# Paced row scatters, paired gathers and column-tiled expert matmuls in an attention and mixture-of-experts kernel

## The chip, the core and the metric

The kernel runs on one core of one Trainium2 chip. The metric is the device time of one execution in microseconds (us); before the change the median of three runs is 681.27 us (680.93 to 682.08).

## What is computed

One transformer layer on x of 1 x 2048 x 128, all in float32. x is normalised, and two branches are added to it.

```
xn = layernorm(x)
attention: 16 heads of width 8; q, k, v = xn W * mod
  w = softmax(q k^T / sqrt(8) * cos(2 pi (i - j) / 2048)) over j
  w = (w + roll(w, 1)) / sqrt(2);  out = (w v) Wo
experts:   logits over 8 experts per token; the best 2 are taken, softmax over the 2
  for each taken pair (token, expert e):
    a, g = split(xn w1[e]^T)       # 352 + 352 columns
    y = (silu(a) * g) w2[e]^T      # 128 columns, times the pair's score
out = x + attention + sum of the token's two y
```

## The kernel before, in words

**Attention** sets the order of the work. 16 heads are taken one after the other. A head has 64 score tiles of 128 keys by 512 queries; a score tile is one f16 matmul of 49 rows (line 1253) into a PSUM bank. Five banks form a ring, filled in groups of 3 and 2 tiles. ACT takes each group with one exponential (line 652) into `probs`. Four finished tiles make a set (a "quad" in the code, w = 0 to 255, 16 to a head), and `weighted_values` (line 1270) multiplies a set with the head's values: four matmuls, each on a column tile of 32 columns of the array, each with a moving operand of 512 columns. A float32 matmul stands in the trace as two, and a float32 transpose as one. Each set raises `pv_done`.

**Rounds** carry everything else. A round is 5 score tiles, so 1.25 sets, and there are 205. In a round PE issues the two score groups, then at most one or two maximum jobs (`max_job`, for the two heads with an exact shift), then one expert step, then the sets that have become ready. `scores(g)` waits until ACT has finished group g - 2.

**Experts.** The 4096 token and expert pairs are sorted by expert into 39 tiles of 128 slots. Slots and owners come from `assign_slots` in round 8. POOL then scatters the normalised rows into slot order in DRAM (`slots_x`, line 550): 32 indirect DMAs of 128 rows. Before the change they come in two runs of 16 with nothing between the DMAs of a run; between the runs POOL waits for `pv_done` of 16 and copies head 2's values into `vh` (line 532). After the last it clears `qe`, which shares memory with the rows (line 557).

Expert tile m takes three steps in three rounds, and two tiles take 7 rounds, from round `EXPERTS_AT` on (`expert_step`): step 0 is `result(m - 1)` (line 1198, 3 matmuls) and `turn_rows(m)` (line 1179, one transpose), steps 1 and 2 are `widen` (line 1189, 3 matmuls each). All of them use the full 128 by 128 array with 128 moving columns. ACT adds one tanh to step 1 (line 644), DVE copies between steps (lines 901 to 923).

**SP** loads each head's operands (`load_head`, 10 DMAs, lines 352 to 401), asks for the first expert rows and weights in its program order at round `EXPERTS_AT` - 2 (lines 410, 429, 430), and for the exact heads' operands at `EXPERTS_AT`.

**Gathers.** The 39 results go to DRAM (`slots_y`). From set `GATHER_AT` on POOL brings them back in token order with 32 indirect DMAs (line 536), one per set, each after `pv_done` of w. DVE adds them in head 15 from its set 4 on, w = 244, and needs all 32.

**Maximum jobs.** 64 of them, `JOBS_A_HEAD` to a head from head `FIRST_JOB_HEAD` on; heads 14 and 15 need the result.

Of the kernel before, what the change touches and what calls it, by code (L numbers as in the profile page):

```python
# [37 lines left out]
P = 128  # L38
S = 2048
DM = 128  # L40
H = 16
D = 8
E = 8
F = 352
NT = S // P
# [23 lines left out]
EXACT = 2  # L69
PLAIN = H - EXACT  # L70
JOBS = EXACT * NT * 2
FIRST_JOB_HEAD = 3
JOBS_A_HEAD = 7
JOB_QUAD = 4
PAIR_EXP_AT = 3
TOP_EXP_AT = 12
RANK_AT = 8
SECOND_AT = 9
EXPERTS_AT = 26
ROUNDS_A_PAIR = 7  # L80
SQUARES_AT = (4, 5)
HALF_HEADS = H // 2
EARLY = HALF_HEADS - EXACT
GATHER_AT = 206
ISQ8 = float(1.0 / np.sqrt(D))
TWO_PI = 2.0 * np.pi
PI_A = 6.28125
# [19 lines left out]
def build(nc, x, Wq, Wk, Wv, Wo, phase, amp, wqkv, w1, w2, ident_in, desc_in, cs_in, sel_in, tri_in, below_in, count_in, heads_in, earlier_in, out):  # L107
# [11 lines left out]
    with ExitStack() as ctx:  # L119
# [393 lines left out]
        def _(pool):  # L513
# [31 lines left out]

            pool.wait_ge(xn_ready, NT)
            pool.wait_ge(slot_ready, 1)
            for r in range(2):
                for t in range(NT):
                    nc.gpsimd.indirect_dma_start(slots_x, bass.IndirectOffsetOnAxis(ap=slot[:, r, t:t + 1], axis=0),  # L550
                                                 xn[:, t, :], None).then_inc(scattered, 16)
                if r == 0:
                    pool.wait_ge(pv_done, QUADS)
                    head_values(2)

            pool.wait_ge(scattered, 2 * NT * 16)
            nc.gpsimd.memset(qe[:], 0.0).then_inc(rows_ready, 1)

            for w in range(2 * QUADS, H * QUADS):
                if w % QUADS == 0 and w // QUADS + 1 < H:  # L560
                    pool.wait_ge(pv_done, w)
                    head_values(w // QUADS + 1)
                j = w - GATHER_AT
                if j == 0:
                    for half in range(2):
                        pool.wait_ge(y_wr[half], ROW_PAIRS // 2 * 16)
                    pool.wait_ge(scratch_wr, 16 * 16)
                    pool.wait_ge(norm_parts, 4)
                if 0 <= j < 2 * NT:
                    pool.wait_ge(pv_done, w)  # L570
                    gather_result(j)

        @block.scalar
        def _(act):
# [490 lines left out]
        def _(pe):  # L1065
# [105 lines left out]
            def turn_rows(m):  # L1171

                pe.wait_ge(xg_ld[m // 2 % 2], m // 4 * 16 + 16)
                after(pe, xgT_ready, m)
                if m == 0:
                    pe.wait_ge(order_ready, 2)
                    pe.wait_ge(slot_ready, 1)
                after(pe, hidT_ready, m)
                nc.tensor.transpose(ps[:, SIDE_BANK, 0:P], xg[:, m % 4, :], ident[:]).then_inc(xgT_ps, 1)  # L1179

            def widen(m, b, ready):

                pe.wait_ge(staged_ld[m % STAGES], (m // STAGES + 1) * 32)
                pe.wait_ge(xgT_ready, m + 1)
                after(pe, y_copied, m)
                if b == 1:
                    pe.wait_ge(a_taken, m + 1)
                for f, (f0, n) in enumerate(FCH):
                    ins = nc.tensor.matmul(ps[0:n, SIDE_BANK, P * f:P * f + P],  # L1189
                                           w1_of[m % STAGES][:, F * b + f0:F * b + f0 + n],  # L1190
                                           xgT[:, m % 2, :], start=True, stop=True)
                ins.then_inc(ready, 1)

            def result(m):
                pe.wait_ge(hidT_ready, m + 1)
                after(pe, y_copied, m)
                for f, (f0, n) in enumerate(FCH):
                    ins = nc.tensor.matmul(ps[:, SIDE_BANK, FP:FP + DM], hidT[0:n, m % 2, f, :],  # L1198
                                           w2_of[m % STAGES][0:n, f, :], start=f == 0, stop=f == NF - 1)
                ins.then_inc(y_ready, 1)  # L1200

            def expert_work(r):
# [210 lines left out]
```

## Time and profile before

| | |
|---|---|
| median of 3 runs | 681.27 us |
| the profiled execution, its own time | 681.02 us |
| its span in the profile | 679.1 us |
| mean granted TensorE clock | 0.961 of full |
| PE busy | 595.2 us, 88% |
| ACT busy | 524.2 us, 77% |
| POOL busy | 81.7 us, 12% |

Times in the trace are microseconds from the start of the span. A row of a timeline is a stretch of instructions of one line: start, length, engine, line, operation, operands, count, and in brackets how long the engine had been idle and what ended that. "remote" or "another core or an unknown queue" means that the event that released the engine could not be matched to an instruction that had just finished. PEld is the loading of weights into the array, which overlaps PE.

### The profile page before, as it was taken

Reading aid. Unit: us, or ns where it says so; the run is one execution under the profiler, and the core shown is the slowest. Engines: PE = TensorE matmul, PEld = TensorE weight load, DVE = VectorE, ACT = ScalarE, POOL = GpSimd, SP = SyncE. Lnnn points to the kernel's source line nnn. Section 1 sums busy time; section 2 is a strip of 40 time slices with the busy share of each in tenths; the row PEclk is TensorE's granted clock in tenths of the full one; section 3 lists DMA queues with packets and bytes.
Section 4 is the critical chain, followed back from the end, with each engine's and each line's share of the span. In section 5 each row is a group of like instructions: output and inputs, shape, how many; then the busy total and the mean of one; then the engine's idle time right before and its main releaser. Section 6 shows DMA issues by size and latency. Waiting matters only on the chain.

```text
span 679.1 us, 11462 instructions
## 1 busy us (share of the span) xinstructions
PE 595.2 (88%) x4181; PEld 209.4 (31%) x4181; DVE 199.2 (29%) x491; ACT 524.2 (77%) x489; POOL 81.7 (12%) x94
## 2 busy tenths in 40 slices
PE   2887766389999999999999999999999998888985
PEld 1341111013333334333333333333333331211213
DVE  6675511002123232323333232332323220000233
ACT  2649945398888788887887888888878889999992
POOL 4100176500000000000000000000000003455000
PEclk9997787599999999999999999999999999999999
DMA  8345122404322224132131322223222100111002
GB/s 236 117 131 171 42 65 67 134 22 130 115 77 82 84 76 117 52 106 68 58 117 60 100 75 84 82 60 99 83 77 82 44 9 21 36 33 34 9 1 65
DMA packets 42813, 52.99 MB, mean 78 GB/s; under 512 B 7245, under 2 KB 32359, under 8 KB 42499
## 3 DMA queue, kind: packets, MB, share of 16 engines
q1 hardware_dynamic: 39616, 47.71, 23.4%
q0 software_dynamic: 2048, 4.20, 2.1%
q8 instruction: 36, 0.59, 0.3%
q10 hardware_dynamic: 1090, 0.30, 0.3%
q14 instruction: 23, 0.18, 0.1%
HBM read 38.54 MB, written 13.63 MB: 77 GB/s over the span
## 4 chain that ended last, share of the span: by engine, by line
PE 58%; ACT 18%; issue 15%; another core or an unknown queue 3%; DVE 2%; DMA 1%; ACTq 1%; SPq 0%; DVEq 0%
PE ps L1270 25%; PE ps L1253 16%; ACT big L652 15%; PE ps L1189 7%; PE ps L1198 5%; ACT cs L644 2%; PE ps L1087 2%; PE ps L1277 1%; PE ps L1287 1%; ACTq L578 1%; PE ps L1179 1%; PE ps L1228 1%; DMA ang<-L_attn_quantum_amplitude 1%; PE ps L1075 1%
## 5 line engine op out<-in xcount | busy, mean ns | idle before, releaser
L652 ACT ACTIVATE big<-ps 128x1536 f32<-128x1536 f32 (+1 forms) x410 | 482.0, 1245 | 114.3 <-PE ps L1253 89.8
L1270 PE MATMUL ps<-big,vh 128*32 128x512 f32 x2048 | 269.5, 616 | 0.0
L1253 PE MATMUL ps<-qa,ka 49*128 49x512 f16 x896 | 164.9, 395 | 52.0 <-ACT big L652 42.0
L1253 PEld LDWEIGHTS ps<-qa,ka 49*128 49x128 f16 x896 | 39.3, 94 | 256.2 <-ACT big L652 221.2
L1189 PE MATMUL ps<-xgT,store 128*128 128x128 f32 (+1 forms) x468 | 72.5, 291 | 0.0
L961 DVE TENSOR_REDUCE m<-ps 128x1 f32<-128x512 f32 x64 | 44.3, 692 | 94.0 <-PE ps L1287 94.0
L1270 PEld LDWEIGHTS ps<-big,vh 128*32 128x32 f32 x2048 | 45.6, 109 | 75.3 <-issue 60.5
L1189 PEld LDWEIGHTS ps<-xgT,store 128*128 128x128 f32 (+1 forms) x468 | 55.7, 181 | 28.2 <-issue 28.2
L532 POOL COPY vh<-vaug 128x144 f32 x16 | 5.1, 319 | 433.8 <-PE ps L1270 407.6
L908 DVE SCALAR_TENSOR_TENSOR cs<-cs,ps 128x384 f32<-128x384 f32 x39 | 21.6, 554 | 75.0 <-ACT cs L644 75.0
L901 DVE COPY xgT<-ps 128x128 f32<-128x128 f32 x39 | 11.4, 292 | 92.0 <-PE ps L1179 92.0
L536 POOL DMA_INDIRECT store<-slots_y,slot x32 | 30.5, 954 | 57.7 <-PE ps L1270 54.5
L550 POOL DMA_INDIRECT slots_x<-attnT,slot x32 | 31.3, 980 | 44.6 <-DVE slot L888 35.1
L1198 PE MATMUL ps<-store,cs 128*128 128x128 f32 (+1 forms) x234 | 36.4, 292 | 0.0
L1198 PEld LDWEIGHTS ps<-store,cs 128*128 128x128 f32 (+1 forms) x234 | 29.0, 190 | 13.3 <-issue 13.3
L917 DVE SCALAR_TENSOR_TENSOR cs<-cs,ps 128x384 f32<-128x384 f32 x39 | 21.6, 554 | 35.5 <-PE ps L1189 35.0
L1253 PE MATMUL ps<-attnT,ka 49*128 49x512 f16 x128 | 24.4, 384 | 7.9 <-ACT big L652 7.0
L944 DVE COPY osb<-ps 128x512 f32<-128x512 f32 x16 | 11.0, 687 | 68.2 <-PE ps L1270 67.5
L1287 PE MATMUL ps<-ka,attnT 49*128 49x512 f16 x64 | 24.1, 376 | 0.0
L644 ACT ACTIVATE cs<-ps 128x384 f32<-128x384 f32 x39 | 18.9, 485 | 0.0
L1087 PE MATMUL ps<-xnT,wmat 128*64 128x512 f32 x64 | 18.6, 677 | 0.0
L1253 PEld LDWEIGHTS ps<-attnT,ka 49*128 49x128 f16 x128 | 5.7, 93 | 38.3 <-ACT big L652 34.4
(164 smaller groups left out, 231.8 us busy)
## 6 DMA issues: line engine op xcount, KB each, us to landing
store<-in_L_ffn_w SPq DMA_DIRECT2D x39, 352.0 KB, 3.0
store<-in_L_ffn_w SPq DMA_DIRECT2D x39, 192.0 KB, 3.1
qk_parts<-store SPq DMA_DIRECT2D x16, 256.0 KB
qa<-qk_parts SPq DMA_DIRECT2D x27, 128.0 KB
slots_x<-vh SPq DMA_DIRECT2D x5, 512.0 KB, 6.2
cs<-slots_x SPq DMA_DIRECT2D x20, 128.0 KB, 3.1
slots_y<-y SPq DMA_DIRECT2D x19, 128.0 KB, 3.1
ka<-qk_parts SPq DMA_DIRECT2D x31, 64.0 KB, 2.2
```

The costliest lines, as they stand in the source:

```text
L536: nc.gpsimd.indirect_dma_start(gathered[:, r, t, :], None, slots_y, bass.IndirectOffsetOnAxis(ap=slot[:, r, t:t + 1], axis=0)).then_inc(ga ...
L550: nc.gpsimd.indirect_dma_start(slots_x, bass.IndirectOffsetOnAxis(ap=slot[:, r, t:t + 1], axis=0), xn[:, t, :], None).then_inc(scattered, 16)
L644: nc.scalar.activation(turned_gate[:, m % 2, :], ps[:, SIDE_BANK, 0:FP], ACT.Tanh, scale=0.5).then_inc(gate_ready, 1)
L652: nc.scalar.activation(probs[:, prob_of(tiles[0]):prob_of(tiles[-1]) + 1, :], ps[:, bank_of(tiles[0]):bank_of(tiles[-1]) + 1, :], ACT.Exp, ...
L908: nc.vector.scalar_tensor_tensor(turned_gate[:, k, :], turned_gate[:, k, :], 1.0, ps[:, SIDE_BANK, 0:FP], ALU.add, ALU.mult).then_inc(a_ta ...
L961: nc.vector.tensor_reduce(m4[:, NT * r + i, c:c + 1], ps[:, O_BANKS[(p - 1) % 2], :], AX, ALU.max).then_inc(m_reduced, 1)
L1087: ins = nc.tensor.matmul(ps[64 * half:64 * half + 64, PROJ_BANKS[n % 4], :], wmat[:, which, 64 * g:64 * g + 64], xnT[:, CW * c:CW * c + CW ...
L1189: ins = nc.tensor.matmul(ps[0:n, SIDE_BANK, P * f:P * f + P], w1_of[m % STAGES][:, F * b + f0:F * b + f0 + n], xgT[:, m % 2, :], start=Tru ...
L1198: ins = nc.tensor.matmul(ps[:, SIDE_BANK, FP:FP + DM], hidT[0:n, m % 2, f, :], w2_of[m % STAGES][0:n, f, :], start=f == 0, stop=f == NF - 1)
L1253: ins = nc.tensor.matmul(ps[:, bank_of(n), :], k[at:at + KQ, P * o:P * o + P], q[at:at + KQ, CW * c:CW * c + CW], start=True, stop=True, t ...
L1270: ins = nc.tensor.matmul(ps[32 * c:32 * c + 32, O_BANKS[p % 2], :], vh[:, p % 2, o + 8 * b, :], probs[:, prob_of(n), :], start=k == 0, sto ...
L1287: nc.tensor.matmul(ps[:, O_BANKS[(p - 1) % 2], :], qe[at:at + KQ, r, P * i:P * i + P], near_keys(ka[at:at + KQ, 2 + r, :], i), start=True, ...
```

## The change

1. The 32 row scatters are issued one by one, each after a further set of value matmuls (w = 16 to 47); the clearing of `qe` follows at w = 48, ahead of head 4's values.
2. Expert steps start in round 41 instead of 26, so that they end in round 177 instead of 162. The maximum jobs go 8 to a head over heads 4 to 11 instead of 7 to a head over heads 3 to 12.
3. Gathers start at set 224 instead of 206, two to a set.
4. Each expert matmul, and the transpose of the rows, becomes several matmuls of 32 columns on the array's four column tiles: a widening step has 4 + 4 + 3 instead of 3, a result 12 instead of 3, the transpose becomes 4 ordinary matmuls with the identity. Per expert tile 38 matmuls stand in place of 10.

```diff
--- before.py
+++ after.py
@@ -69,19 +69,21 @@
 EXACT = 2
 PLAIN = H - EXACT
 JOBS = EXACT * NT * 2
-FIRST_JOB_HEAD = 3
-JOBS_A_HEAD = 7
+FIRST_JOB_HEAD = 4
+JOBS_A_HEAD = 8
 JOB_QUAD = 4
 PAIR_EXP_AT = 3
 TOP_EXP_AT = 12
 RANK_AT = 8
 SECOND_AT = 9
-EXPERTS_AT = 26
+EXPERTS_AT = 41
+SCATTER_AT = 16
 ROUNDS_A_PAIR = 7
 SQUARES_AT = (4, 5)
 HALF_HEADS = H // 2
 EARLY = HALF_HEADS - EXACT
-GATHER_AT = 206
+GATHER_AT = 224
+GATHERS_A_QUAD = 2
 ISQ8 = float(1.0 / np.sqrt(D))
 TWO_PI = 2.0 * np.pi
 PI_A = 6.28125
@@ -545,22 +547,23 @@
 
             pool.wait_ge(xn_ready, NT)
             pool.wait_ge(slot_ready, 1)
-            for r in range(2):
-                for t in range(NT):
-                    nc.gpsimd.indirect_dma_start(slots_x, bass.IndirectOffsetOnAxis(ap=slot[:, r, t:t + 1], axis=0),
-                                                 xn[:, t, :], None).then_inc(scattered, 16)
-                if r == 0:
-                    pool.wait_ge(pv_done, QUADS)
-                    head_values(2)
-
-            pool.wait_ge(scattered, 2 * NT * 16)
-            nc.gpsimd.memset(qe[:], 0.0).then_inc(rows_ready, 1)
-
-            for w in range(2 * QUADS, H * QUADS):
+            def scatter_rows(j):
+                r, t = j // NT, j % NT
+                nc.gpsimd.indirect_dma_start(slots_x, bass.IndirectOffsetOnAxis(ap=slot[:, r, t:t + 1], axis=0),
+                                             xn[:, t, :], None).then_inc(scattered, 16)
+
+            for w in range(SCATTER_AT, H * QUADS):
+                i = w - SCATTER_AT
+                if i < 2 * NT:
+                    pool.wait_ge(pv_done, w)
+                    scatter_rows(i)
+                if i == 2 * NT:
+                    pool.wait_ge(scattered, 2 * NT * 16)
+                    nc.gpsimd.memset(qe[:], 0.0).then_inc(rows_ready, 1)
                 if w % QUADS == 0 and w // QUADS + 1 < H:
                     pool.wait_ge(pv_done, w)
                     head_values(w // QUADS + 1)
-                j = w - GATHER_AT
+                j = GATHERS_A_QUAD * (w - GATHER_AT)
                 if j == 0:
                     for half in range(2):
                         pool.wait_ge(y_wr[half], ROW_PAIRS // 2 * 16)
@@ -568,7 +571,8 @@
                     pool.wait_ge(norm_parts, 4)
                 if 0 <= j < 2 * NT:
                     pool.wait_ge(pv_done, w)
-                    gather_result(j)
+                    for k in range(GATHERS_A_QUAD):
+                        gather_result(j + k)
 
         @block.scalar
         def _(act):
@@ -1176,7 +1180,10 @@
                     pe.wait_ge(order_ready, 2)
                     pe.wait_ge(slot_ready, 1)
                 after(pe, hidT_ready, m)
-                nc.tensor.transpose(ps[:, SIDE_BANK, 0:P], xg[:, m % 4, :], ident[:]).then_inc(xgT_ps, 1)
+                for c in range(0, DM, 32):
+                    ins = nc.tensor.matmul(ps[c:c + 32, SIDE_BANK, 0:P], xg[:, m % 4, c:c + 32], ident[:], start=True, stop=True,
+                                           tile_position=(0, c))
+                ins.then_inc(xgT_ps, 1)
 
             def widen(m, b, ready):
 
@@ -1186,17 +1193,19 @@
                 if b == 1:
                     pe.wait_ge(a_taken, m + 1)
                 for f, (f0, n) in enumerate(FCH):
-                    ins = nc.tensor.matmul(ps[0:n, SIDE_BANK, P * f:P * f + P],
-                                           w1_of[m % STAGES][:, F * b + f0:F * b + f0 + n],
-                                           xgT[:, m % 2, :], start=True, stop=True)
+                    for c in range(0, n, 32):
+                        ins = nc.tensor.matmul(ps[c:c + 32, SIDE_BANK, P * f:P * f + P],
+                                               w1_of[m % STAGES][:, F * b + f0 + c:F * b + f0 + c + 32],
+                                               xgT[:, m % 2, :], start=True, stop=True, tile_position=(0, c))
                 ins.then_inc(ready, 1)
 
             def result(m):
                 pe.wait_ge(hidT_ready, m + 1)
                 after(pe, y_copied, m)
                 for f, (f0, n) in enumerate(FCH):
-                    ins = nc.tensor.matmul(ps[:, SIDE_BANK, FP:FP + DM], hidT[0:n, m % 2, f, :],
-                                           w2_of[m % STAGES][0:n, f, :], start=f == 0, stop=f == NF - 1)
+                    for c in range(0, P, 32):
+                        ins = nc.tensor.matmul(ps[c:c + 32, SIDE_BANK, FP:FP + DM], hidT[0:n, m % 2, f, c:c + 32],
+                                               w2_of[m % STAGES][0:n, f, :], start=f == 0, stop=f == NF - 1, tile_position=(0, c))
                 ins.then_inc(y_ready, 1)
 
             def expert_work(r):
```

## Rows read from the trace of the kernel before

**Rows 1.** the page: engines' busy time, granted clock in 40 slices, chain that ended last.
```profile
...
PE 595.2 (88%) x4181; PEld 209.4 (31%) x4181; DVE 199.2 (29%) x491; ACT 524.2 (77%) x489; POOL 81.7 (12%) x94
...
PEclk9997787599999999999999999999999999999999
...
PE 58%; ACT 18%; issue 15%; another core or an unknown queue 3%; DVE 2%; DMA 1%; ACTq 1%; SPq 0%; DVEq 0%
```

**Rows 2.** waits between 60 and 140 us: total us, times, longest.
```profile
...
ACT big L652 <- remote: 24.2, 4, 13.2
...
DVE weight_sums L952 <- remote: 15.0, 1, 15.0
DVE rank L775 <- remote: 9.7, 1, 9.7
```

**Rows 3.** timeline 72 to 136 us (start, length, engine, line), and one window's sums.
```profile
...
80.91 1.16 POOL L550 DMA_INDIRECT slots_x<-attnT,slot  x1 [35.15 <-DVE slot L888]
...
90.56 0.39 PE L1253 MATMUL ps<-qa,ka 49*128 49x512 f16 x2 [0.31 <-issue]
...
94.60 1.45 ACT L652 ACTIVATE big<-ps 128x1536 f32<-128x1536 f32 x1 [4.10 <-remote]
...
100.18 1.18 POOL L550 DMA_INDIRECT slots_x<-attnT,slot  x1 [0.30 <-issue]
...
105.53 0.98 POOL L550 DMA_INDIRECT slots_x<-attnT,slot  x1 [0.34 <-issue]
...
115.26 0.82 PE L1253 MATMUL ps<-qa,ka 49*128 49x512 f16 x5
...
124.61 0.96 POOL L550 DMA_INDIRECT slots_x<-attnT,slot  x1 [0.30 <-issue]
...
128.38 2.37 ACT L652 ACTIVATE big<-ps 128x1536 f32<-128x1536 f32 x2 [13.21 <-remote]
...
106.00:130.00 24.00, 10.70 (x66) 2.26 (x64) 1.14 (x6) 9.21 (x9) 18.11 (x17) 0.71 0.21 66
```

**Rows 4.** windows, ACT's line 652 alone: one stretch with, one without expert steps.
```profile
...
163.00:557.00 394.00, 312.04 (x264) 1.00 0.27 81
563.00:655.00 92.00, 85.59 (x76) 1.00 0.09 24
```

**Rows 5.** timeline 300 to 322 us, PE: value, widening and result matmuls.
```profile
...
300.45 1.92 PE L1270 MATMUL ps<-big,vh 128*32 128x512 f32 x16
...
303.05 0.93 PE L1189 MATMUL ps<-xgT,store 128*128 128x128 f32 x6
...
303.91 1.06 PE L1270 MATMUL ps<-big,vh 128*32 128x512 f32 x8
...
305.68 0.94 PE L1198 MATMUL ps<-store,cs 128*128 128x128 f32 x6
...
306.66 1.07 PE L1270 MATMUL ps<-big,vh 128*32 128x512 f32 x8
```

**Rows 6.** the same timeline at 81.8 us: the densest matmuls of the trace.
```profile
...
81.82 0.54 PE L1108 MATMUL ps<-sel,second 128*128 128x8 bf16 x16 [2.00 <-DVE sel L749]
```

**Rows 7.** SP's issues of one head's load (timeline), and median landing times (page).
```profile
...
301.06 0.33 SPq L352 DMA_DIRECT2D qa<-qk_parts  x1
...
305.21 0.24 SPq L401 DMA_DIRECT2D qa<-shift_rows  x1
...
store<-in_L_ffn_w SPq DMA_DIRECT2D x39, 352.0 KB, 3.0
...
cs<-slots_x SPq DMA_DIRECT2D x20, 128.0 KB, 3.1
```

**Rows 8.** timeline, POOL: gathers at one to a set of value matmuls.
```profile
...
594.51 0.95 POOL L536 DMA_INDIRECT store<-slots_y,slot  x1 [1.31 <-PE ps L1270]
595.76 0.95 POOL L536 DMA_INDIRECT store<-slots_y,slot  x1 [0.30 <-issue]
597.11 0.95 POOL L536 DMA_INDIRECT store<-slots_y,slot  x1 [0.40 <-PE ps L1270]
```

## The prediction

> **What bounds the kernel now.** I read the page first. PE is busy 88% of the span, ACT 77%, and the chain that ended last is 58% PE and 18% ACT [rows 1]. So matmuls set the time, but not everywhere, and 3% of the chain belongs to nobody: "another core or an unknown queue". The granted clock is at 9 tenths or more in 35 of 40 slices and lower in slices 4 to 8, about 51 to 136 us [rows 1]. Two questions follow: what happens there, and what sets the pace of a round elsewhere.
>
> The waits of 60 to 140 us answer the first. ACT stands still 24.2 us in 4 waits whose releaser is unknown, and DVE 15.0 and 9.7 us in one wait each [rows 2]. The timeline tells who is late. The scores of 90.56 us are done in 0.39 us, yet ACT takes them at 94.60; the scores of 115.26 us are taken at 128.38, 13.21 us of idle ACT [rows 3]. DVE's two waits are for PE as well. So a signal that PE sends arrives microseconds late. What runs beside it is POOL's scatters: 16 in a row from 80.91 to about 101.4, and 16 from 105.53 to 125.6, at a pitch of 1.27 us ((100.18 - 80.91) / 15 is 1.28) [rows 3]. The first stall begins some 10 us after its run of scatters began, the second likewise, and the last one ends 2.8 us after the last scatter. My reading: scatters that follow each other without a pause hold up PE's signals after about eight of them. Around the stalls PE also runs at a reduced clock, 0.71 on average from 106 to 130 us [rows 3], though slice 4 shows that the clock was low before the first scatter.
>
> For the second question I count ACT's exponentials, two to a round. With expert steps 132 rounds take 394 us, 2.98 us each; without, 38 rounds take 92 us, 2.42 each, and there ACT's line 652 alone is busy 85.6 of 92 [rows 4]. So rounds without expert work are ACT's, those with it are PE's, and an expert step costs time because it stands in PE's order between scores and value matmuls.
>
> **The scatters.** Spaced, they need a pitch of one set. A round is 1.25 sets, so a set is 2.42 / 1.25 = 1.94 us; POOL's 1.27 us fits. The gathers of the kernel before have just that spacing, with at most three in a row (594.51, 595.76, 597.11) [rows 8], and no unknown wait stands beside them. So the stalls should go: ACT's 24.2 less some 0.7 that it would have idled anyway, **-23.5 us**. Bounds: 0 if spacing does not help, -24.2. With no stall the clock should recover sooner: PE was busy 10.7 us at 0.71 in one window [rows 3], of which full clock saves at most 3.1, and the first stall is like it; between 0 and 6 I take **-2**, as half of the slow matmuls stood beside ACT's work and the clock was low before. What waits instead: `vh` of heads 2 and 3 is copied after one scatter of 1 us, and is needed 16 sets (31 us) later; the clearing of `qe` at w = 48 and head 4's copy behind it have the same 31 us, and the exact heads' operands are wanted only in round 55. All cost nothing while rounds take 2.4 us.
>
> **The later start of the experts.** The same 137 rounds carry them. The maximum jobs lie in 8 heads instead of 10; each needs PE's place in a round and its count stays 64. Between 0 and 2 us I take **+1**. New is that the first rows are wanted soon after the last scatter. Count from the start T of round 38. SP first waits for its first score group (0.6), reads a register (about 1), and issues head 4's ten DMAs, which take 4.4 us [rows 7]. The last scatter starts when set 46 is done, T + 2, and has landed by T + 4.4, so SP, not POOL, is late. The rows are asked for at T + 6 and land 3.1 us later [rows 7], at T + 9; PE wants them in round 41 after its scores, 3 x 2.42 + 0.8 = T + 8.1. The first weights (3.0 us to land [rows 7]) come behind them, at T + 11, wanted at T + 10.5. PE waits once for about 1 us, between 0 and 3: **+1**. Its sets and ACT queue behind that wait.
>
> **The gathers.** They must be in by w = 244 and start at w = 224. Two of them are 2.5 us (0.95 + 0.30 each [rows 8]) against 1.94 us of a set, so POOL falls behind and works 40 us without a pause; 20 sets are 39 us. They land 3 us after DVE could begin adding. 32 additions of 0.3 us, about 10, then still end before head 15 does at w = 256, 23 us after w = 244. By itself that costs 0. What a pauseless run may do is a rival below.
>
> **The column tiles.** Now 6 full-array matmuls of a widening step start at 303.05 and the next value matmuls at 303.91: 0.86 us. A result with the transpose of the next rows takes 305.68 to 306.66: 0.98 [rows 5]. The value matmuls show what column tiles do. One set is eight matmuls of 512 columns in 1.06 us, two sets 1.92, so four matmuls on four column tiles advance together at 0.86 / 2 = 0.43 us [rows 5]. With 128 columns, four should take a quarter, 0.107; I take 0.109. The widening step becomes 3 chunks x 2 passes = 6 such groups: 0.65, and 0.02 for the first load, 0.68. That is no faster as arithmetic: the full array paces at the same rate. What goes is the switch: in a step's last 0.2 us the array drains before the value matmuls can load; in the same tiling they follow at once, and their own first load (0.02) hides too. Saved per widening step 0.86 - 0.68 + 0.02 = 0.20. The result has 6 groups too, but the transpose grows from one pass to two: 0.68 + 0.22 = 0.90, saved 0.98 - 0.90 + 0.02 = 0.10. PE saves 78 x 0.20 + 39 x 0.10 = 19.5 us.
>
> Not all of it shows. Per two tiles (7 rounds) expert steps take PE 4 x 0.86 + 2 x 0.98 = 5.4 us, but the rounds are longer by only 7 x 0.56 = 3.9, or 72% of it: ACT's pace hides the rest. I take 70%, **-14 us**; all of it would be -19.5, none 0.
>
> **Sum.** The profiled execution took 681.0 us (span 679.1 and 1.9 around it), within 0.3 of the median of 681.3. 681.0 - 23.5 - 2 + 1 + 1 - 14 = 643.5, and against the median 644.
>
> **Rivals.**
> (a) *The paired gathers bring the stall back.* POOL then issues 32 without a pause, as in the scatters' runs. For: same kind of instruction, same pitch of 1.25 to 1.27 us [rows 3, 8]. Against: they write to the core, not to DRAM, and POOL waits for PE before each pair, so a stall throttles its own cause. Worked out: PE goes on for 9 us (4.6 sets), POOL needs 11.5 for their pairs, and signals recover some 2 us after it stops. About 4.6 us are lost for 4.6 sets, three times in 16 sets: 14 us, **658**.
> (b) *Spaced scatters stall PE too*, as the cause is the scatters' number and not their pitch. Half of the stalls left: **656**; all: 669.
> (c) *The column tiles save nothing.* The densest matmuls here are 16 in 0.54 us, 0.034 each with its load [rows 6]. If that is the floor, a widening step's 22 take 0.75 (saved 0.1) and result and turn, 32, take 1.09 (lost 0.1): PE saves 4 us, 3 show, **655**.
> (d) *PE's issue becomes the bound: slower.* The 0.034 was seen over 16 pairs only, which may have been queued while PE stood still; over a longer stretch the trace shows no more than 8 pairs in 0.86 us, 0.107 each [rows 5]. 39 tiles issue 39 x (2 x 22 + 32) = 2964 pairs where 105 us were spent. At x us a pair the steps cost 2964 x - 105; at 0.044 this eats the scatters' 25.5, beyond it the kernel is slower. Taken at 0.05: 681 - 25.5 + 43 + 2 = **701**. Against: rows 5's second set follows at the array's pace, and rows 6.
>
> The Trainium skill, "TensorE: Matmul & The Clock Gate", section "Wait — 56ns, not 53.3ns?", says that with hardware decoding off the sequencer spends about 62 ns on each matmul, which binds once the array's work per matmul is shorter. By that page 2964 pairs would be 184 us, an estimate, and the kernel would take about 736 us; the 0.034 of rows 6 speaks against it.
> (e) *The change does not do what it says*, say the sets no longer line up with the expert steps or a load comes much later than I count: 5 us or more on top.
>
> **How the numbers follow.** Forecast (643.5 to 644, own range 637 to 650) 0.48; (a) 0.24; (b) 0.10; (c) 0.09; (d) 0.05; (e) 0.04. The low end takes the whole 19.5 us of PE and a bit more clock: 637, with 1 to spare 636. The high end must hold (a), (b) at half and (c), with their spread: 664. Outside are (d), the full (b) and part of (e). About 0.2% (1.4 us) is what can be told from no change. All cases but (d) are faster by far: faster 0.94, same 0.01, slower 0.05. The predicted time is the likeliest case's, 644.
>
> **What the changed profile would show.** Scatters right: one per 1.9 us, no unknown wait of ACT, and a clock above 0.83 from 100 us on. Widening right: 22 matmul records (44 a tile), six groups at 0.11 us, and value matmuls 0.68 us after the step's start; at 1 us or more (d) is true, at 0.75 (c). Rounds with expert steps should take 2.88 us, those without 2.42. A wait of PE for rows or weights of about 1 us stands at round 41. In the gathers' stretch the round tells (a): 2.42, or over 2.9 with unknown waits. The prediction is wrong if the sets do not follow an expert step at once, if scatters at a pitch of 1.9 us still delay PE's signals, or if the saved PE time turns into waits for ACT.

## The result, and the profile after

| | before | after |
|---|---|---|
| median | 681.56 us of 4 runs (680.93 to 682.08) | 658.24 us of 4 runs (657.71 to 662.35) |
| ratio | | 0.967, 95% interval 0.963 to 0.971 |
| the profiled execution | 681.02 us | 657.95 us |
| its span | 679.1 us | 656.0 us |

The kernel is 23.3 us faster. That lies inside the predicted range (636 to 664), but not at the likeliest case, 644: it is the number of rival (a), 658.

The page of the kernel after: busy times, clock in 40 slices of 16.4 us, POOL's slices, the chain that ended last.

```profile
PE 576.5 (88%) x6404; PEld 211.0 (32%) x6404; DVE 202.2 (31%) x491; ACT 523.8 (80%) x489; POOL 81.6 (12%) x94
...
POOL 4200014445000000000000000000000000266200
PEclk9987789999999999999999999999999999977999
...
PE 56%; ACT 19%; issue 17%; DMA 2%; SPq 2%; DVE 2%; ACTq 1%; another core or an unknown queue 1%; DVEq 0%
```

Against [rows 1]: PE has 2223 more matmuls and is busy 18.7 us less. The 3% of the chain that belonged to nobody are now 1%. The clock's dip ahead of 98 us (slices 3 to 6) is still there; a second one has appeared in slices 36 and 37 (574 to 607 us), under POOL's second busy stretch. That is where to look.

First the two stretches that the change was meant for. Waits of 60 to 140 us: the largest of POOL and DVE, and ACT's only line (total us, times, longest):

```profile
POOL slots_x L552 <- PE ps L1279: 69.8, 18, 49.0
...
DVE osb L948 <- PE ps L1279: 24.1, 1, 24.1
...
ACT big L656 <- PE ps L1262: 6.5, 8, 1.3
```

No wait there has an unknown releaser any more; [rows 2] had 24.2 us of them on ACT alone. The sums of 98 to 140 us, of before and of after, show the same (each fence: busy us and count of each engine, then granted clock, DMA share, GB/s):

```profile
98.00:140.00 42.00, 22.77 (x130) 4.49 (x132) 5.45 (x19) 19.45 (x17) 22.05 (x21) 0.69 0.29 91
```

```profile
98.00:140.00 42.00, 36.91 (x261) 7.99 (x259) 1.96 (x7) 38.25 (x34) 20.13 (x23) 1.00 0.16 48
```

34 exponentials in place of 17. The granted clock is 1.00 (2.4 GHz) in place of 0.69; in the trace before it stood at 0.50 (1.2 GHz) from 97 to 110 us, after ACT's first wait, and again from 121 to 134, in the longest wait and behind it.

The column tiles, in PE's timeline of a widening step and of a result with its transpose:

```profile
298.99 0.75 PE L1197 MATMUL ps<-xgT,store 128*32 128x128 f32 x19
299.47 0.62 PE L1279 MATMUL ps<-big,vh 128*32 128x512 f32 x1
299.56 0.28 PE L1197 MATMUL ps<-xgT,store 128*32 128x128 f32 x3
299.67 1.89 PE L1279 MATMUL ps<-big,vh 128*32 128x512 f32 x15
...
304.87 0.86 PE L1207 MATMUL ps<-store,cs 128*32 128x128 f32 x24
305.55 0.40 PE L1184 MATMUL ps<-ident,cs 128*32 128x128 f32 x8
305.77 1.04 PE L1279 MATMUL ps<-big,vh 128*32 128x512 f32 x8
```

The widening step has 22 records and gives way to the value matmuls after 299.67 - 298.99 = 0.68 us, where it took 0.86 [rows 5]; result and transpose take 305.77 - 304.87 = 0.90, where they took 0.98. Both are the numbers of the prediction. One value matmul even starts at 299.47, inside the step: the last chunk of 96 columns uses three column tiles, which leaves the fourth to it (that it is the fourth is inferred; the rows do not name the tile).

Then the exponentials of ACT's line 656 in three windows (two to a round): with expert steps, beside the gathers, and behind them.

```profile
170.00:555.00 385.00, 314.48 (x267) 1.00 0.28 83
564.00:612.00 48.00, 32.13 (x28) 0.86 0.16 42
614.00:638.00 24.00, 22.82 (x21) 1.00 0.02 4
```

385 / 133.5 is 2.88 us a round, as forecast. Behind the gathers it is 24 / 10.5 = 2.3 (2.42 was forecast; the window's edges cut rounds, and 12 whole rounds, 192 to 204, take 2.44 each). Between them stands what the forecast's likeliest case did not have: 48 us for 14 rounds, 3.4 us each. Fourteen rounds should take 34. The waits of 560 to 656 us name it:

```profile
ACT big L656 <- remote: 9.5, 4, 3.3
...
POOL store L538 <- remote: 6.7, 3, 2.4
```

And the timeline of the first of these waits, all engines, with some rows left out:

```profile
573.21 2.37 ACT L656 ACTIVATE big<-ps 128x1536 f32<-128x1536 f32 x2 [0.34 <-PE ps L1262]
...
574.72 0.60 PE L1262 MATMUL ps<-attnT,ka 49*128 49x512 f16 x3 [0.33 <-issue]
...
575.63 0.39 PE L1262 MATMUL ps<-attnT,ka 49*128 49x512 f16 x2 [0.31 <-ACT big L656]
576.05 0.95 POOL L538 DMA_INDIRECT store<-slots_y,slot  x1 [0.30 <-issue]
577.31 0.95 POOL L538 DMA_INDIRECT store<-slots_y,slot  x1 [0.30 <-issue]
578.48 1.45 ACT L656 ACTIVATE big<-ps 128x1536 f32<-128x1536 f32 x1 [2.90 <-remote]
578.57 0.95 POOL L538 DMA_INDIRECT store<-slots_y,slot  x1 [0.30 <-issue]
579.83 0.95 POOL L538 DMA_INDIRECT store<-slots_y,slot  x1 [0.30 <-issue]
...
582.99 0.95 POOL L538 DMA_INDIRECT store<-slots_y,slot  x1 [2.21 <-remote]
```

The group of three score tiles begun at 574.72 (128x1536 for ACT) is done by about 575.3. ACT, idle from 575.58, takes it at 578.48. The group of two begun at 575.63 is done by about 576.0, and ACT takes it at 580.58, 4.6 us later. The gathers began at 568.44 and follow each other every 1.26 us; the tenth starts at 579.83, and then POOL itself waits for PE's late signal. ACT and POOL are released together, at 582.90 and 582.99, some 2 us after the tenth gather ended. The trace also keeps the semaphores' updates: four of PE's, for work that had ended up to several us earlier, come within 0.2 us there (582.73 to 582.92). So the signals look queued: they come late and one by one while the gathers run, and in a burst once POOL pauses. The trace has four such runs (10, 10, 10 and 2 gathers) and three stalls, beginning six or seven gathers into a run: the picture of [rows 3], cut into pieces.

The stall has a second price. Behind the first two of the three, PE runs at half clock (0.50, which is 1.2 GHz) for a while; it had been busy for 3.5 of the 7 us from 575 to 582, ahead of the first such stretch. A part of that stretch, with all engines (the other is 596 to 602.5 us):

```profile
583.00:588.00 5.00, 4.45 (x20) 0.66 (x17) 0.00 (x0) 4.62 (x4) 3.80 (x4) 0.50 0.14 39
```

To see where all of the 23 us went I counted rounds by the starts of ACT's exponentials in four traces: before and after; the kernel after on another chip (e16, below); and before with the column tiles alone (e2, below). Microseconds of each stretch (rounded, so sums can be 0.1 off):

| rounds | before | after | e2, tiles alone | e16, after on another chip |
|---|---|---|---|---|
| 0 to 8 | 25.8 | 25.2 | 25.7 | 25.7 |
| 8 to 20, the scatters | 60.0 | 33.7 | 33.5 | 38.2 |
| 20 to 178, all expert steps | 461.4 | 449.3 | 449.0 | 449.3 |
| 178 to 182 | 9.8 | 10.9 | 9.8 | 11.0 |
| 182 to 192, gathers paired | 24.4 | 38.5 | 24.4 | 24.4 |
| 192 to 204 | 29.3 | 29.3 | 29.3 | 29.3 |

Before to after: -0.6 - 26.3 - 12.1 + 1.1 + 14.1 = -23.8; the first exponential came 0.7 us later, so -23.1, which is the difference of the spans. The change won 38.4 us in two places and gave 14.1 back in ten rounds. ACT's unknown waits are 9.5 of the 14.1; most of the rest is ACT waiting for PE with a known releaser, where PE runs at half clock and catches up (ACT is idle 14.7 us in these ten rounds, and 1.6 before).

### The profile page after: what moved, and what is told of

Its sections match the earlier page's. It is cut to its first block, busy times and chain, and to the rows that moved or that the text cites. A ratio compares the mean times of both kernels' runs of the same rounds, so it can differ in the third digit from the quotient of the medians.

```text
span 656.0 us, 15907 instructions
## 1 busy us (share of the span) xinstructions
PE 576.5 (88%) x6404; PEld 211.0 (32%) x6404; DVE 202.2 (31%) x491; ACT 523.8 (80%) x489; POOL 81.6 (12%) x94
## 3 DMA queue, kind: packets, MB, share of 16 engines
q1 hardware_dynamic: 39616, 47.71, 24.4%
## 4 chain that ended last, share of the span: by engine, by line
PE 56%; ACT 19%; issue 17%; DMA 2%; SPq 2%; DVE 2%; ACTq 1%; another core or an unknown queue 1%; DVEq 0%
PE ps L1279 23%; PE ps L1262 16%; ACT big L656 16%; PE ps L1197 5%; PE ps L1207 5%; ACT cs L648 2%; PE ps L1091 2%; PE ps L1184 1%; PE ps L1286 1%; PE ps L1296 1%; ACTq L582 1%; PE ps L1237 1%; PE ps L1079 1%; PE ps L1101 1%
## 5 line engine op out<-in xcount | busy, mean ns | idle before, releaser
L1279 PE MATMUL ps<-big,vh 128*32 128x512 f32 x2048 | 280.8, 610 | 0.0
L1279 PEld LDWEIGHTS ps<-big,vh 128*32 128x32 f32 x2048 | 65.6, 109 | 52.2 <-issue 43.5
L1197 PE MATMUL ps<-xgT,store 128*32 128x128 f32 x1716 | 66.8, 277 | 0.4 <-DMA store<-in_L_ffn_w 0.4
L1197 PEld LDWEIGHTS ps<-xgT,store 128*32 128x32 f32 x1716 | 45.8, 109 | 27.9 <-issue 27.2
L1262 PE MATMUL ps<-attnT,ka 49*128 49x512 f16 x128 | 26.0, 414 | 17.6 <-ACT big L656 12.7
L1207 PE MATMUL ps<-store,cs 128*32 128x128 f32 (+1 forms) x936 | 33.7, 277 | 0.0
L921 DVE SCALAR_TENSOR_TENSOR cs<-cs,ps 128x384 f32<-128x384 f32 x39 | 21.6, 555 | 33.5 <-PE ps L1197 31.7
L1207 PEld LDWEIGHTS ps<-store,cs 128*32 128x32 f32 (+1 forms) x936 | 23.3, 110 | 13.2 <-issue 13.2
```

Source lines behind the costliest of these rows:

```text
L1197: ins = nc.tensor.matmul(ps[c:c + 32, SIDE_BANK, P * f:P * f + P], w1_of[m % STAGES][:, F * b + f0 + c:F * b + f0 + c + 32], xgT[:, m % 2, ...
L1207: ins = nc.tensor.matmul(ps[c:c + 32, SIDE_BANK, FP:FP + DM], hidT[0:n, m % 2, f, c:c + 32], w2_of[m % STAGES][0:n, f, :], start=f == 0, s ...
L1262: ins = nc.tensor.matmul(ps[:, bank_of(n), :], k[at:at + KQ, P * o:P * o + P], q[at:at + KQ, CW * c:CW * c + CW], start=True, stop=True, t ...
L1279: ins = nc.tensor.matmul(ps[32 * c:32 * c + 32, O_BANKS[p % 2], :], vh[:, p % 2, o + 8 * b, :], probs[:, prob_of(n), :], start=k == 0, sto ...
```

## The experiments

Twelve runs were made. They fell on several chips, and it turned out that the chip matters, so each time stands beside that of the kernel before on the same chip.

**1. The whole change without the column tiles.**

```diff
...
-                for c in range(0, DM, 32):
-                    ins = nc.tensor.matmul(ps[c:c + 32, SIDE_BANK, 0:P], xg[:, m % 4, c:c + 32], ident[:], start=True, stop=True,
-                                           tile_position=(0, c))
-                ins.then_inc(xgT_ps, 1)
+                nc.tensor.transpose(ps[:, SIDE_BANK, 0:P], xg[:, m % 4, :], ident[:]).then_inc(xgT_ps, 1)
...
```

(`widen` and `result` go back likewise.)

> The kernel after, with the transpose, the widening and the result matmuls of the experts back on the full array (10 matmuls a tile instead of 38). If column tiles save what the prediction says (0.20 us of PE per widening step, 0.10 per result, 70% of it shown), this takes 14 us more than the kernel after: about 672, and rounds with expert steps 2.98 instead of 2.90 us. If the column tiles save nothing (rival c) it takes 655 to 660, the same as the kernel after.

Measured: 656.88 us against 655.48 of before, ratio 1.003 (0.9995 to 1.006). The surprise is the second number: the kernel before, 681 us in the result, took 655 here. On this chip the stalls do not exist (the traces of 2 and 3 show it), and all of the change but the tiles is worth nothing. The forecast of 14 us between this kernel and the one after was borne out in part by experiment 3, on the same chip and with the same tiles and start of the experts as after: 645.21, 11.7 us less, and 13.4 us less in rounds 20 to 178 (449.3 against 462.7). With expert steps a round took 3.00 us:

```profile
170.00:555.00 385.00, 304.33 (x257) 1.00 0.29 85
```

**2. The column tiles alone**, put into the kernel before: the reverse of that edit.

> The kernel before with the column tiles alone. By the forecast 14 us less than before: about 667. If the gain depends on the other parts, or is nothing: 678 to 681. The stalls of 90 to 128 us stay as they were (ACT idle on unknown releasers about 24 us).

Measured on the same chip: 641.23 against 655.48, ratio 0.977 (0.974 to 0.980): -14.3 us. A round with expert steps, 330 / 114.5 = 2.88 us:

```profile
170.00:500.00 330.00, 269.05 (x229) 1.00 0.28 84
```

Its scatters still come in two runs of 16, at the pitch of [rows 3]. Here are their first ones, and the sums of the stretch that holds both runs:

```profile
82.68 0.98 POOL L550 DMA_INDIRECT slots_x<-attnT,slot  x1 [0.30 <-issue]
83.96 0.97 POOL L550 DMA_INDIRECT slots_x<-attnT,slot  x1 [0.30 <-issue]
```

```profile
80.00:126.00 46.00, 39.27 (x286) 8.77 (x289) 8.48 (x31) 42.76 (x39) 34.17 (x34) 0.96 0.21 66
```

ACT is busy 42.8 of 46 us, with no unknown wait. The same scatters, on another chip, cause no stall: a pauseless run of indirect DMAs does not suffice for it.

**3. The scatters back in two runs of 16, all else as after.**

```diff
-                if i < 2 * NT:
+                if i < 2 * NT and i % NT == 0:
                     pool.wait_ge(pv_done, w)
-                    scatter_rows(i)
+                    for k in range(NT):
+                        scatter_rows(i + k)
```

> The kernel after, with the 32 row scatters in two runs of 16 again (at sets 16 and 32). If it is the pauseless run that holds up PE's signals, two stalls come back beside them, 11 to 13 us each, and the time is 658 + 23 to 26 = 681 to 684. If it was the place in the kernel (the early rounds, their table loads and head order) that stalled and not the run, 658 to 661.

Measured: 645.21, ratio 0.985 (0.980 to 0.990), on the chip of the first two. No unknown wait in the scatters nor in the paired gathers, although all 32 gathers follow each other at 1.26 us here, in one row. A miss: it was written for a chip that stalls, and says nothing of the pitch. It took 4.0 us more than experiment 2, of which the later start explains 1.5 (below); its four times spread from 642.9 to 648.5, and the rest is not explained.

**4. One gather to a set.** So that they can start at set 204, the expert steps are packed into 6 rounds for two tiles in place of 7.

```diff
-ROUNDS_A_PAIR = 7
+ROUNDS_A_PAIR = 6
-GATHER_AT = 224
-GATHERS_A_QUAD = 2
+GATHER_AT = 204
+GATHERS_A_QUAD = 1
```

> The kernel after, with an expert step in every round (two tiles in 6 rounds instead of 7), so that the experts end 19 rounds earlier, and the gathers one to a set from set 204 on. If the paired gathers' pauseless run costs the 14 to 15 us of rival (a), this takes 642 to 644, with no unknown wait of ACT or POOL after 540 us. If the rounds of the last heads are slow for another reason (DVE's late additions, the exact heads), 655 to 658. If the denser expert steps cost more than the free rounds hid: 645 to 650.

Measured, still on that chip: 640.31, ratio 0.976 (0.972 to 0.979). Without stalls on the chip this does not tell the expectation's cases apart; it does show that the denser packing costs nothing (rounds 41 to 182 take 405.2 us, against 407.8 in experiment 3). The tiles alone (experiment 2) took 641.23 there, so on such a chip nearly all of the gain is theirs.

**5 and 6. After and before again, on another chip**, to find out whether the stalls are real and which chips have them.

> The kernel after, unchanged, since the kernel before took 655.5 us on the chip of the first four experiments and 681.6 on the chip of the result, and no unknown wait stood in their traces. If the stalls belong to some chips and not to others: on a chip where before takes 655, after takes 641 to 644, a ratio of 0.98, with no unknown waits beside its gathers; on a chip where before takes 681, after takes 658, ratio 0.967. If the gathers' stall is there on every chip: 655 to 658 even where before takes 655.

> The kernel before, unchanged, for its trace on this chip. If it takes 655: ACT has no wait on an unknown releaser between 80 and 130 us although the scatters stand in the same two runs of 16 at a pitch of 1.27 us, and rounds 8 to 20 take 33 to 34 us instead of 60. If it takes 681: the same stalls as in the first trace.

Measured: after 661.38, before 680.35, ratio 0.973 (0.969 to 0.978); before once more, 679.7. This chip stalls. Rounds 182 to 204 of the kernel after take 69.5 us in its trace, where a trace without stalls has 53.8: the gathers cost 15.7 us. Waits beside the gathers of the kernel after, then waits of 60 to 140 us of the kernel before:

```profile
ACT big L656 <- remote: 10.8, 3, 4.7
```

```profile
ACT big L652 <- remote: 24.8, 3, 13.2
DVE weight_sums L952 <- remote: 14.2, 1, 14.2
DVE rank L775 <- remote: 7.4, 1, 7.4
```

They are the sizes of the result's chip, so the stall is not chance. It goes with the chip: the experiments ran on five chips; three had the kernel before at 655 to 658 us, and no trace from them has such a wait; two had it at 680. (Whether the result's chip is one of these two is not known. Each chip was used in one session only, so the chip itself and its state in that session are not told apart.)

**7 and 8. One gather to a set, and gathers in two pauseless runs of 16**, both packed as in 4. The edit of 8, against 4:

```diff
...
-                if 0 <= j < 2 * NT:
+                if 0 <= j < 36 and j % 18 == 0:
                     pool.wait_ge(pv_done, w)
-                    for k in range(GATHERS_A_QUAD):
-                        gather_result(j + k)
+                    for k in range(16):
+                        gather_result(j // 18 * 16 + k)
```

> The same kernel as e4_single_gathers (an expert step in every round, gathers one to a set from set 204 on), since its first run fell on a chip without stalls. On a chip where before takes 680: if the paired gathers' pauseless run is the whole cause of the last stretch's loss, 641 to 644 and no unknown wait, a ratio of 0.943 to 0.947; if single gathers stall this chip too, 650 or more. On a chip where before takes 655: 640 again.

> The kernel of e4_single_gathers, but the gathers in two runs of 16 without a pause, at sets 204 and 222: as the scatters stood before, and at the same mean rate as single gathers. On a chip where before takes 680: if the length of a pauseless run is the cause, two stalls of ACT of about 11 us each, starting 6 to 10 us into each run, 662 to 668; if the mean rate is what counts, no stall, 641 to 644. On a chip where before takes 655: no stall, 640.

Measured: 642.25 against 658.18, ratio 0.977 (0.971 to 0.982), and 644.98 in a single run. The chip had no stalls, so 8 settles nothing.

**9. One gather to a set, a third time**, now on a chip that stalls (before 680.48).

> The same kernel as e4_single_gathers once more, as both runs of it fell on chips without stalls. Where before takes 680: 641 to 644 if every pauseless run is gone and single transfers don't stall (ratio 0.943 to 0.947), 650 or more if single ones do. Where before takes 655: 640 to 642.

Measured: 640.08, ratio 0.945 (0.938 to 0.952). No unknown wait in the whole trace. The stretch of the gathers:

```profile
530.00:610.00 80.00, 74.81 (x66) 1.00 0.10 25
```

80 / 33 = 2.42 us a round. On chips that stall, the kernel after lost 14 to 16 us in its gathers. POOL still issues up to four gathers in a row (behind the copy of `vh`), which is short enough:

```profile
532.53 0.97 POOL L538 DMA_INDIRECT store<-slots_y,slot  x1 [0.34 <-issue]
533.81 0.96 POOL L538 DMA_INDIRECT store<-slots_y,slot  x1 [0.30 <-issue]
535.07 0.95 POOL L538 DMA_INDIRECT store<-slots_y,slot  x1 [0.30 <-issue]
536.33 0.95 POOL L538 DMA_INDIRECT store<-slots_y,slot  x1 [0.30 <-PE ps L1279]
538.93 0.95 POOL L538 DMA_INDIRECT store<-slots_y,slot  x1 [1.65 <-PE ps L1279]
```

**10. Four patterns in one kernel**, on that chip: a pauseless run of 16 scatters, 16 scatters one to a set, 16 gathers with a small POOL operation (a memset of unused memory) behind each, and two pauseless runs of 8 gathers. Whichever stalls then stalls beside one that doesn't. The part of the edit on the gathers:

```diff
...
+                if j == 0:
+                    pool.wait_ge(pv_done, w)
+                    for k in range(NT):
+                        gather_result(k)
+                        nc.gpsimd.memset(pause[:, k, :], 0.0)
+                if j in (20, 30):
                     pool.wait_ge(pv_done, w)
-                    for k in range(GATHERS_A_QUAD):
-                        gather_result(j + k)
+                    for k in range(8):
+                        gather_result(NT + 8 * (j // 30) + k)
```

> The kernel of e4_single_gathers with four different spacings in one look. Scatters: 16 in a run at set 16, the other 16 one to a set from set 32. Gathers: 16 in a run at set 204, each followed by a POOL memset of some 0.4 us, so at a pitch of about 1.7 us; 8 in a run at set 224; 8 in a run at set 234. On a chip where before takes 680, if a pauseless run of more than about seven is the cause: unknown waits of ACT beside the scatters' run (about 11 us), none beside the scatters one to a set, none or up to 4 us beside each run of 8. If the pitch matters and not the number, none beside the paused gathers; if the number without a wait in between matters, about 11 us there too. On a chip where before takes 655: no unknown waits, 640 to 645.

Measured, a single run: 664.57 us. The pauseless scatters (97.96 to 118.2) hold ACT up twice. Timeline:

```profile
109.62 0.96 POOL L553 DMA_INDIRECT slots_x<-attnT,slot  x1 [0.30 <-issue]
110.77 2.36 ACT L666 ACTIVATE big<-ps 128x1536 f32<-128x1536 f32 x2 [5.76 <-remote]
110.89 0.96 POOL L553 DMA_INDIRECT slots_x<-attnT,slot  x1 [0.30 <-issue]
...
119.27 1.45 ACT L666 ACTIVATE big<-ps 128x1536 f32<-128x1536 f32 x1 [6.13 <-remote]
```

The windows of ACT's line 666 (busy, count, clock, DMA share, GB/s): pauseless scatters, scatters one to a set, paced gathers.

```profile
98.00:120.00 22.00, 10.10 (x10) 0.79 0.18 58
141.00:172.00 31.00, 28.58 (x26) 1.00 0.15 49
540.00:565.00 25.00, 23.27 (x21) 1.00 0.15 40
```

4.4 us a round in the first, 2.38 in the others. The paced gathers are the telling ones. POOL issues 16 of them without waiting for anybody, busy nearly all the time. What differs from the two runs of 8 gathers is the memset between them, and with it the pitch, 1.57 us:

```profile
544.09 0.45 POOL L581 MEMSET pause<- 128x400 bf16 x1
544.71 0.96 POOL L539 DMA_INDIRECT store<-slots_y,slot  x1 [0.16 <-issue]
```

No unknown wait stands beside them. Each run of 8 at 1.26 us has one again, 2.6 and 2.7 us (waits of 575 to 600 us):

```profile
ACT big L666 <- remote: 2.6, 1, 2.6
```

So on one chip, in one execution: 16 at 1.27 us stall (11.9 us), 8 at 1.26 stall a little (2.7), 16 at 1.57 do not, nor at one to a set. Sixteen do no harm when they are spaced, and both scatters and gathers do harm when they are not: how densely they come decides, and a longer dense row costs more. Whether it is the pitch or the other operation in between that helps, the memset does not tell apart.

The unknown waits are not the whole cost. Against experiment 9 on the same chip, rounds 8 to 20 take 49.3 us in place of 33.7 (15.6 more, with 11.9 of unknown waits) and rounds 182 to 204 take 62.9 in place of 53.8 (9.1 more, with 5.3). Behind each of the two runs of 8 the granted clock falls to 0.50: it is that from 592.2 to 598.8 and from 616 to 622.7 us, where experiment 9 has 1.00 throughout its gathers.

**11 and 12. The kernel after with such a pause behind each gather, and the kernel after once more.**

```diff
...
                     for k in range(GATHERS_A_QUAD):
                         gather_result(j + k)
+                        nc.gpsimd.memset(pause[:, j + k, :], 0.0)
```

> The changed kernel with one edit: after every gather POOL also clears 128 x 340 unused elements, which should take about 0.39 us, so that the gathers follow each other at about 1.5 us (0.96 + 0.39 + 0.16) and not 1.26; the pairs stay, POOL is busy without a break for about 48 us from w = 224 on. Pitch theory: no unknown waits of ACT or POOL beside the gathers, rounds there near 2.42 us, and on a chip whose kernel before takes about 680 us a time of 643 to 646, against 658 to 661 for the changed kernel. Theory that the two gathers to a set, or POOL without a break, are the cause: the stalls stay, 656 or more. On a chip whose kernel before takes about 656 us there is nothing to stall and both theories expect 643 to 646; the run then says only that the pause costs nothing. DVE's additions end some 10 us later than before, still ahead of head 15's last set.

> The changed kernel again, unedited, on the same chip as e15. If the kernel before takes about 680 us here: 658 to 661, with unknown waits of ACT of about 10 us beside the gathers. If the kernel before takes about 656 us here: no unknown waits, and 642 to 645, since e1 (all of the change but the tiles) took what the kernel before took and the tiles alone saved 14.

Measured: 645.34 and 645.57 against 657.30, both ratio 0.981 (0.976 to 0.987); a chip without stalls, no unknown wait in either. So the cure of the kernel after by this pause alone is not shown where it would count; that the pause costs nothing is. What 12 gives is the last column of the table above: the kernel after, unedited, on such a chip. Its 32 gathers come in one row at 1.26 us, as nothing holds POOL up. From round 20 to 204 it repeats the result's trace to 0.1 us in every stretch but one, rounds 182 to 192: 24.4 against 38.5. The paired gathers cost 14.1 us on the result's chip, and nothing else differs there. (Behind round 204 it is 1.2 us slower.) It is 4.5 us slower in rounds 8 to 20, before any gather. The sums of 75 to 97 us show a lower clock there, 0.72, where the result's trace has 0.88; it comes with some of the executions, this one taking 648.0 us while two of its four runs took 643.

```profile
75.00:97.00 22.00, 18.93 (x116) 4.75 (x113) 8.60 (x31) 15.79 (x15) 0.00 (x0) 0.72 0.05 16
```

```profile
75.00:97.00 22.00, 19.08 (x137) 4.76 (x134) 9.35 (x33) 19.38 (x19) 1.50 (x2) 0.88 0.12 31
```

## Why the prediction was right and where it was wrong

**What bounds the kernel: right.** "A signal that PE sends arrives microseconds late" while POOL issues indirect DMAs without a pause: the stalls left with the pauseless scatters, and came where pauseless gathers were put. One row was misread, without effect: the exponential of 94.60 us takes three score tiles, so it belongs to the group of three that PE began at 89.64, and not to the two of 90.56; its signal is later than the text says. What the prediction could not see is that this is so on some chips only; the trace of before came from one of them, as did the result.

**The scatters, -23.5 and -2 for the clock: right.** Rounds 8 to 20 are 26.3 us shorter, against 25.5, and the clock stands at 1.00 from 98 to 140 us, where it had been at 0.50 for much of the time. The two terms were not measured apart. The bound of 0 was for "spacing does not help", rival (b); experiment 10 (e14) excludes it, with no unknown wait beside 16 scatters one to a set on a chip where the pauseless ones lost 11.9 us. On chips without stalls the term is 0 (33.5 us for these rounds in e2 with both runs in place, 33.7 after).

**The later start, +1, and the wait for the first load, +1: a little less, right in kind.** PE waited for the first weights as said, for 0.40 us. The row, the first widening step, in round 42:

```profile
165.89 0.75 PE L1197 MATMUL ps<-xgT,store 128*32 128x128 f32 x19 [0.40 <-DMA store<-in_L_ffn_w]
```

Rounds 20 to 182 take 460.2 us in after and 458.7 in e2, which differ there by the later start and the packing of the maximum jobs: +1.5 for both terms.

**The column tiles, -14: right.** -14.3 us as a pair of medians in e2, -12.5 (461.42 to 448.96) by its rounds 20 to 178 against those of before, on two chips, and -13.4 by the same rounds of e3 against e1, on one chip. The steps took 0.68 and 0.90 us to the hundredth, and a round 2.88. With e1's 3.00 a round on the chip of e2's 2.88, 137 x 0.12 is 16. Rival (c) would have given 3 us; rival (d), slower, fell with the 44 records of a tile's widening steps: 22 in 0.68 us are 0.031 each, where it needed 0.044.

Counted in matmuls as the code has them, each of which stands as two records, result and transpose are 16 in 0.90 us, 0.056 each, and rows 6 had 0.034. The Trainium skill's ("TensorE: Matmul & The Clock Gate", section "Wait — 56ns, not 53.3ns?") 62 ns a matmul with hardware decoding off is longer than either, so that case does not hold here. That what was saved is the drain at the change of the array's shape is argued: the step's end came 0.18 us sooner at equal arithmetic, but the tiles also made each weight load a quarter as wide, and no run tells the two apart.

**The gathers, 0: this is the step that failed.** The text says: "POOL falls behind and works 40 us without a pause ... By itself that costs 0", and leaves what a pauseless run may do to rival (a), with a chance of 0.24. It cost 14.1 us in rounds 182 to 192. The prediction's own reading of [rows 3], that indirect DMAs without a pause hold up PE's signals after about eight of them, applied to 32 gathers at the same pitch, and its own sum said that POOL would run without a pause. The reasons "against" were of two kinds. That gathers write to the core and not to DRAM made no difference. That POOL waits for PE and so throttles the stall was true (the 2.1 to 2.4 us of POOL's late signals), but that was already in the 14 us. With that step at 14.1 the sum is 643.5 + 14.1 = 657.6, and the profiled execution took 657.95.

**The rival's working** held in its outline: "About 4.6 us are lost for 4.6 sets, three times in 16 sets". The trace has three stalls, in runs of ten gathers; the runs begin 14.6 us apart (568.44, 582.99, 597.61), where ten gathers' five sets should take 9.7, so 4.9 are lost each time. What makes them up is partly something else. PE's signals came in time for 7 us and not 9, the unknown waits of ACT are about 3 us a stall, and the drop of the clock behind a stall, which the working did not have, is in the rest. That the sum came to 14 as well is in part luck.

**What would have been better:** one gather to a set from set 204 on, with the experts packed to 6 rounds for two tiles: 640.1 us on a chip that stalls, where before took 680.5, and 640.3 and 642.3 on two that don't, against 655.5 and 658.2. It beats both kernels on each kind of chip. Of its 18.0 us of span against the result's 656.0, rounds 182 to 204 make 14.1, the stall; rounds 41 to 182, in which it differs by the packing, 2.8 (405.0 against 407.8), and the stretch ahead of them, where the two kernels do the same, 1.3. The packing was not tried alone.

## What to carry to other kernels

Look at the density of what one engine issues, not only at its busy time: POOL was busy for 12% of the span and, on the chips that stall, cost 24 us, then 14. Space the indirect DMAs that POOL issues: waits for other work between them were enough in experiment 9, and a POOL operation of 0.45 us behind each in experiment 10. When a stall's cause has been read from a trace, hold every part of the change against the same reading before any of them is costed at nothing; and run before and after on more than one chip, since a gain of 23 us on one can be 12 on another.

Small matmuls that stand between matmuls of a column tiling gained from taking the same tiling even at equal arithmetic: 0.18 us for a widening step here, by the prediction's reading the change of the array's shape.

## What the runs showed of the hardware that was not expected

- The same kernel takes 680 to 682 us on some chips (the result's and two of the experiments', of which one may be the same) and 655 to 658 on three others, and the difference stands beside POOL's dense indirect DMAs: rounds 8 to 20 take 60.0 us in before's trace and 33.5 in that of e2, which scatters in the same way.
- Such waits were seen with 8 or more of POOL's indirect DMAs in a row at a pitch of 1.26 to 1.27 us (2.7 us for a run of 8, up to 13 for 16), scatters to DRAM and gathers to the core alike; not at 1.57 us, nor where at most four came in a row between waits for sets (e12). A short pause does not always end them: in e5 a run of ten gathers, 1.39 us of waiting and four more were followed by another late signal to POOL, and a wait of ACT lasted right through the pause (580.08 to 584.82).
- It is what PE sends that is late, to ACT, DVE and POOL; ACT's signal to PE is not: in the timeline of the first stall ACT's exponentials end at 573.21 + 2.37 = 575.58 and PE's scores start at 575.63. The late signals end in a burst (four in 0.2 us) some 2 us after POOL pauses.
- A stall costs more than its waits: after PE had stood waiting in it, the granted clock was 0.50 (583 to 588 and 596 to 602.5 us in after, 592.2 to 598.8 and 616 to 622.7 in e14, 97 to 110 and 121 to 134 in before). The third stall of after had no such drop (1.00 from 605 to 615 us).
- A chunk of 96 columns in column tiles leaves the fourth tile free, and the next value matmul starts 0.2 us early, by inference on that tile.

What stays open: why some chips stall and others don't, what holds PE's signals (the ends of matmuls are modelled in the trace, so that their results come late and not only the signals is not excluded), whether the pitch or the operation in between helps, and if the pitch, where between 1.27 and 1.57 us the limit lies.
